# In each head, the output products of the head in front move ahead of the attend products

## Chip, cores, metric

The kernel runs on one core of one Trainium2 chip. The metric is the device time of one execution in microseconds; lower is better. The engines are named as in the profile: PE (TensorE, with PEld for its weight loads), DVE (VectorE), ACT (ScalarE), POOL (GpSimd) and SP, which here only issues transfers.

## What is computed

One transformer layer in float32: layer norm, causal attention with rotary embedding, residual; then layer norm, a mixture of experts (8 experts, the best 2 of each token) with a shared expert, residual. There are 8 sequences of 256 tokens, width 256, 16 heads of 128.

```python
x = x + attn(layernorm(x), wq, wk, wv, wo)      # x: (8, 256, 256)
x = x + moe(layernorm(x), gate_w, w1, w3, w2, sw1, sw3, sw2)

def attn(x, wq, wk, wv, wo):
    q, k, v = (einsum('bsd,dnh->bsnh', x, w) for w in (wq, wk, wv))
    q, k = rope(q) / sqrt(128), rope(k)
    logits = where(causal, einsum('bqnh,bknh->bnqk', q, k), -1e30)
    a = einsum('bnqk,bknh->bqnh', softmax(logits), v)
    return einsum('bqnh,nhd->bqd', a, wo)
```

## The kernel before

Every engine has its own stream of instructions, written out by hand, and semaphores between them; no scheduler reorders anything. An engine works through its stream in order, so what stands behind a wait waits too. To keep float32 accuracy at the speed of the fp32r format, operands are split into a high and a low part: ACT copies the rounded high part out of PSUM, DVE subtracts it to get the low part, and PE does three products (low by high, high by high, high by low; the helper `three`, L638 to L643) where one would do.

The attention stage goes through the sequences b = 0 to 7 and in each through the heads h = 0 to 15, as `sequence(b)` on each of PE, DVE, ACT and POOL. It is a software pipeline: in the turn of head h, PE does

1. `transpose_probs(h)` (L681): three transposes of the softmax rows, after `prob_done` from ACT;
2. `scores(h+2)` (L674, L641), after `qkt_lo` from POOL;
3. `project(h+4)`: q and k of that head, 12 matmuls, and half of one values unit, 3 matmuls of 512 columns; here and there a small product for the router of the sequence in front (`turn_rows` at h = 4, `gate_scores` at h = 5, `ranks` at h = 10), or the transposes of the next sequence's input (h = 11);
4. `attend(h)`: three matmuls `bank<-pt_*,v_*` (L641) and one float32 matmul of two passes, `bank<-pt_late,v_late` (L690), after `pt_lo` from DVE;
5. `output(h-1)`: six matmuls `bank<-w_*,att_*` (L641), which add the product of the head in front with `wo` to the bank of the sequence's output, after `o_lo` from DVE.

The other engines in the turn of head h, each in this order:

- ACT: `pt_late` (L1449) and `pt_hi` (L1450), the copies of the transposed probabilities; `qkt_high(h+3)` (L1425); `normalise(h+1)` (L1437, L1438), which waits for `inv_done`, DVE's reciprocal; `exps(h+2)` (L1432); a values copy in odd heads; then `att_hi` of head h (L1465), which waits for `o_ps`, the end of attend(h); then the high parts of weight pieces (`split_hi`, L1415) and the router's copies, `rows_turned` (L1494) at h = 4.
- DVE: `pt_lo` (L1038, the low part that attend(h) waits for); `rinv` (L1030); mask and maximum of head h+2 (L1026); `rope_cosines` and `rope_sines` of head h+4 (L1010, L1017); `value_lo` in every fourth head (L1035); `att_lo` of head h (L1043), which waits for `att_hi`; then the router's parts, the norms (`rows_norm`, L1142, at h = 2) and low parts of weight pieces (`split_lo`, L984, in sequence 0).
- POOL: the sum of the rope products (L472) and the low part of q and k (L1638), weight pieces, and the scatter of rows to the experts.

In heads 12 to 15 of the last sequence PE has no next sequence to project. There it takes the first products of the shared expert: `up_s(0,0)` in head 12; `up_s(0,1)` and `up_s(1,0)` in head 13; `turn_s(0)` and `up_s(1,1)` in head 14; `up_s(2,0)` and `turn_s(1)` in head 15. These stand where projections stood, ahead of `attend(h)`. ACT does the silu for them (`silu_s`, L1513) behind `att_hi`, with a load of another function table each time it changes between exp and silu. DVE does the products with the gate (`mult_s`, L1188), the low parts (L1194) and the plan of expert tiles (`plan_tiles`, L1284 to L1292) there. After head 15 follow `residual` (L1125), the last sequence's router and 39 expert tiles, then the rest of the shared expert and the sums.

Of the kernel before, what the change touches and what calls it, by code (L numbers as in the profile page):

```python
# [18 lines left out]
N, H = 16, 128  # L19
# [46 lines left out]
def build(nc, x, wq, wk, wv, wo, gate_w, w1, w3, w2, sw1, sw3, sw2, cos_t, sin_t, mask_t, ident_t,  # L66
          order_t, base_t, own_t, route_t, plan_t, zero_t, out):
    ctx = ExitStack()
    with ctx:
# [200 lines left out]
        o_lo = sem("o_lo")  # L270
# [73 lines left out]
        def wait_pieces(eng, n):  # L344

            for who in range(2):
                wait(eng, w_lo[who], lo_count(n, who))
# [116 lines left out]
        def wait(eng, s, value):  # L464

            if not isinstance(value, int) or value > 0:
                eng.wait_ge(s, value)
# [169 lines left out]
        def _(pe):  # L637
# [55 lines left out]
            def output(h):  # L693


                for t in range(ST):
                    mm = three(p_y[:, t, :], [att[h % 2][b][:, t * P:(t + 1) * P] for b in range(2)],
                               [wos(b)[:, h, :] for b in range(2)], h == 0 and t == 0,
                               h == N - 1 and t == ST - 1, more=True)
                mm.then_inc(y_ps, 1)  # L700

            def sequence(b):
                j0 = b * N
                for h in range(N):
# [47 lines left out]
                    if b is not FIRST and h in (4, 5):  # L752
                        pe.wait_ge(max_done[1], j0 + h + 3)
                        if h == 4:
                            turn_rows(b, 0)
                        if h == 5:
                            gate_scores(b, 0)
                    pe.wait_ge(pt_lo, j0 + h + 1)
                    if h % GH == 0:
                        pe.wait_ge(v_lo, b * 4 + h // GH + 1)  # L760
# [2 lines left out]
                    if b is not FIRST and h == 10:  # L763
                        pe.wait_ge(max_done[1], j0 + h + 3)
                        ranks(b, 0)
                    if h >= 1 or b is not FIRST:
                        pe.wait_ge(o_lo, j0 + h)
                        if h == 1:
                            wait(pe, resid_done, b)
                        if b is FIRST and h in (1, 5, 9, 13):  # L770
                            wait_pieces(pe, (14, 22, 30, 32)[h // 4])
                        output((h - 1) % N)
                if b is LAST:
                    pe.wait_ge(o_lo, j0 + N)
                    output(N - 1)
# [9 lines left out]
            def gate_scores(n, a):  # L785
                pe.wait_ge(xt2_cp, n)
                for t in range(ST):
                    for c in range(DC):
                        mm = pe.matmul(p_gate[a][:, t, :], xt2[:, t * DC + c, :], gate_t[:, c, :], start=c == 0,  # L789
                                       stop=c == DC - 1)  # L790
                mm.then_inc(gate_ps, 1)
# [1074 lines left out]
```

## Time and profile before

| | |
|---|---|
| median of 3 runs | 759.54 us (759.2 to 760.19) |
| the profiled execution | 760.51 us, span 758.5 us |
| busy: PE, PEld, DVE | 722.3, 683.8, 643.2 us |
| busy: ACT, POOL | 538.3, 512.7 us |
| attention stage | from about 24 us to about 614 us of the span |
| mean granted TensorE clock | 0.993 of full speed |

The page of the profile gives busy time by engine and, for each engine, how long it stood still ahead of a group of instructions and who released it. PE is above 95% busy, so the question for each wait on it is whether it stands on the path. The heads are followed in the timeline: a turn of a head is taken from the first transpose of its probabilities (`bank<-ident,work`, L681) to the next head's. A matmul's start is a good mark, its end is modelled, and matmuls overlap; 256 columns start 0.12 us apart at full clock.

### The profile page before, as it was taken

To read this page: it belongs to the slowest core of one execution; us is meant where nothing else is said; L and a number is where in the kernel's file an instruction comes from. 1 tells how busy PE (TensorE), PEld (TensorE's weight loads), DVE (VectorE), ACT (ScalarE), POOL (GpSimd) and SP (SyncE) were. 2 spreads that over 40 slices of the span, in tenths; PEclk is the share of its full clock that TensorE was granted. 3 is DMA by queue.
4 is the path that set the end of the run, shared out by engine and by line. 5 is a ranking of instruction groups with operands and counts; after the bars stand their busy time and mean duration, and the time that the engine had idled before them with its cause. 6 is when DMAs were issued, how large, how long until landed. Compare 5 with 4: busy or idle time off the path is not lost.

```text
span 758.5 us, 16245 instructions
## 1 busy us (share of the span) xinstructions
PE 722.3 (95%) x5403; PEld 683.8 (90%) x5403; DVE 643.2 (85%) x1826; ACT 538.3 (71%) x1685; POOL 512.7 (68%) x536
## 2 busy tenths in 40 slices
PE   4899999999999999999999999999999789899998
PEld 4787999999999999999999999999999678699898
DVE  6898889988998989898989988998889557588667
ACT  4788777777777777777778777777776735466574
POOL 5778567777778777877777778777766405445363
PEclk9999999999999999999999999999999999899999
DMA  6545203321332143223302321312444532344371
GB/s 204 147 157 150 96 29 112 116 103 35 122 107 93 37 137 122 72 65 131 136 27 89 126 97 35 101 47 92 175 178 161 209 104 78 112 133 134 119 277 65
DMA packets 49483, 85.91 MB, mean 113 GB/s; under 512 B 8440, under 2 KB 40152, under 8 KB 47800
## 3 DMA queue, kind: packets, MB, share of 16 engines
q1 hardware_dynamic: 45352, 73.44, 28.9%
q0 software_dynamic: 4048, 11.42, 4.2%
q8 instruction: 44, 0.72, 0.4%
q14 instruction: 39, 0.32, 0.1%
HBM read 60.12 MB, written 44.59 MB: 138 GB/s over the span
## 4 chain that ended last, share of the span: by engine, by line
PE 77%; DVE 11%; ACT 5%; POOL 3%; issue 2%; DMA 1%; SPq 0%; another core or an unknown queue 0%; POOLq 0%; DVEq 0%; ACTq 0%
PE bank L641 59%; PE bank L681 4%; PE bank L674 3%; PE bank L690 3%; DVE work L1017 3%; POOL work L472 1%; DVE work L1010 1%; PE bank L885 1%; PE bank L895 1%; PE bank L897 1%; PE bank L866 1%; ACT work L1432 1%; PE bank L789 1%; POOL qkt_lo L1638 1%; DVE work L1026 1%
## 5 line engine op out<-in xcount | busy, mean ns | idle before, releaser
L1638 POOL TENSOR_TENSOR qkt_lo<-work,qkt_hi 128x512 fp32r<-128x512 f32 x128 | 166.1, 1298 | 84.5 <-ACT qkt_hi L1425 84.5
L472 POOL TENSOR_TENSOR work<-work 128x512 f32<-128x512 f32 x127 | 165.2, 1301 | 49.1 <-DVE work L1017 46.1
L1017 DVE TENSOR_TENSOR work<-bank,sinn 64x512 f32<-64x512 f32 x256 | 176.2, 688 | 3.4
L1425 ACT CAST qkt_hi<-work 128x512 fp32r<-128x512 f32 x128 | 79.6, 622 | 97.1 <-POOL work L472 95.1
L641 PE MATMUL bank<-xnt_hi,w_lo 128*128 128x256 f32 x512 | 145.9, 285 | 2.3 <-DVE xnt_lo L1048 2.3
L641 PE MATMUL bank<-xnt_lo,w_hi 128*128 128x256 f32 x512 | 145.5, 284 | 0.0
L641 PE MATMUL bank<-xnt_hi,w_hi 128*128 128x256 f32 x512 | 145.5, 284 | 0.0
L1432 ACT ACTIVATE work<-work,bias 128x128 f32<-128x128 f32 (+1 forms) x256 | 112.7, 441 | 0.0
L1010 DVE TENSOR_TENSOR work<-bank,cosn 128x512 f32<-128x512 f32 x128 | 88.0, 688 | 18.1 <-PE bank L641 17.5
L641 PEld LDWEIGHTS bank<-xnt_hi,w_lo 128*128 128x128 f32 x512 | 98.6, 193 | 3.1 <-DVE xnt_lo L1048 3.1
L641 PEld LDWEIGHTS bank<-xnt_hi,w_hi 128*128 128x128 f32 x512 | 98.9, 193 | 0.0
L641 PEld LDWEIGHTS bank<-xnt_lo,w_hi 128*128 128x128 f32 x512 | 98.8, 193 | 0.0
L641 PE MATMUL bank<-w_hi,att_lo 128*128 128x256 f32 x256 | 83.1, 325 | 0.0
L641 PE MATMUL bank<-w_hi,xnt_hi 128*128 128x512 f32 (+1 forms) x256 | 81.5, 359 | 0.0
L1026 DVE CUSTOM_DVE_ANT_0 work<-bank,mask 128x128 f32<-128x128 f32 (+1 forms) x256 | 78.7, 345 | 1.1 <-PE bank L641 1.1
L641 PE MATMUL bank<-w_hi,xnt_lo 128*128 128x512 f32 (+1 forms) x192 | 71.9, 375 | 4.8 <-DVE xnt_lo L1182 3.5
L641 PE MATMUL bank<-w_lo,att_hi 128*128 128x256 f32 x256 | 72.5, 283 | 0.0
L641 PE MATMUL bank<-w_hi,att_hi 128*128 128x256 f32 x256 | 72.3, 282 | 0.0
L1043 DVE TENSOR_TENSOR att_lo<-bank,att_hi 128x256 fp32r<-128x256 f32 x128 | 54.1, 422 | 21.4 <-ACT att_hi L1465 18.5
L1038 DVE TENSOR_TENSOR pt_lo<-bank,pt_hi 128x256 fp32r<-128x256 f32 x128 | 53.4, 417 | 13.3 <-ACT pt_hi L1450 12.2
L681 PE MATMUL bank<-ident,work 128*128 128x128 f32 x384 | 63.1, 272 | 0.7 <-ACT work L1438 0.6
L1438 ACT ACTIVATE work<-work,rinv 128x256 f32<-128x256 f32 x128 | 63.3, 495 | 0.0
(183 smaller groups left out, 2123.8 us busy)
## 6 DMA issues: line engine op xcount, KB each, us to landing
rows_by_expert<-in_zero_t SPq DMA_DIRECT2D x17, 1028.0 KB
weights_split<-stage SPq DMA_DIRECT2D x40, 176.0 KB, 1.9
w_lo<-weights_split SPq DMA_DIRECT2D x4, 1408.0 KB
stage<-rows_by_expert SPq DMA_DIRECT2D x39, 128.5 KB
w_lo<-results_by_token SPq DMA_DIRECT2D x16, 256.0 KB, 5.5
w_hi<-weights_split SPq DMA_DIRECT2D x2, 1536.0 KB
stage<-in_L_ffn_w SPq DMA_DIRECT2D x32, 88.0 KB
weights_split<-stage SPq DMA_DIRECT2D x20, 128.0 KB, 1.9
```

What stands on the lines that cost most here:

```text
L472: eng.tensor_tensor(roped[:, a], rope_cos[:, a], rope_sin[:, a], ALU.add).then_inc(rope_add, 1)
L641: mm = pe.matmul(out, lhs[a], rhs[b], start=start and n == 0, stop=stop and n == 2, skip_group_check=more)
L681: mm = pe.transpose(p_t[:, k, :], prob[h % 2][:, k * P:(k + 1) * P], ident[:, :])
L1010: nc.vector.tensor_tensor(rope_cos[:, a], p_qk[a][:, :, :], c, ALU.mult)
L1017: op = nc.vector.tensor_tensor(rope_sin[lo:lo + 64, a], p_qk[a][hi:hi + 64, :, :], sn, ALU.mult)
L1026: nc.vector.tensor_tensor_reduce(prob[a][:, cols], p_s[a][:, t, keys], mask[:, m], -SCALE, BIG, ALU.add, ALU.min, bias[:, a, t:t + 1]).the ...
L1038: nc.vector.tensor_tensor(pts[1][:, :, :], p_t[:, 0:2, :], pts[0][:, :, :], ALU.subtract).then_inc(pt_lo, 1)
L1043: nc.vector.tensor_tensor(att[a][1][:, :], p_o[:, a, :], att[a][0][:, :], ALU.subtract).then_inc(o_lo, 1)
L1425: nc.scalar.copy(qkt[a][0][:, :, :], roped[:, a]).then_inc(qkt_hi, 1)
L1432: nc.scalar.activation(prob[a][:, c], prob[a][:, c], ACT.Exp, bias=bias[:, a, t:t + 1], scale=-1.0, accum_out=rsum[:, a, t:t + 1]).then_in ...
L1438: nc.scalar.activation(prob[a][:, P:3 * P], prob[a][:, P:3 * P], ACT.Copy, scale=rinv[:, a, 1:2]).then_inc(prob_done, 1)
L1638: nc.gpsimd.tensor_tensor(qkt[a][1][:, :, :], roped[:, a], qkt[a][0][:, :, :], ALU.subtract).then_inc(qkt_lo, 1)
```

## The change

In PE's `sequence`, the block with the wait for `o_lo` and `output(h-1)` moves from behind `attend(h)` to ahead of it and of its wait for `pt_lo`. Nothing is added or removed, and the streams of DVE, ACT, POOL and SP are the same.

```diff
@@ -755,6 +755,13 @@
                             turn_rows(b, 0)
                         if h == 5:
                             gate_scores(b, 0)
+                    if h >= 1 or b is not FIRST:
+                        pe.wait_ge(o_lo, j0 + h)
+                        if h == 1:
+                            wait(pe, resid_done, b)
+                        if b is FIRST and h in (1, 5, 9, 13):
+                            wait_pieces(pe, (14, 22, 30, 32)[h // 4])
+                        output((h - 1) % N)
                     pe.wait_ge(pt_lo, j0 + h + 1)
                     if h % GH == 0:
                         pe.wait_ge(v_lo, b * 4 + h // GH + 1)
@@ -763,13 +770,6 @@
                     if b is not FIRST and h == 10:
                         pe.wait_ge(max_done[1], j0 + h + 3)
                         ranks(b, 0)
-                    if h >= 1 or b is not FIRST:
-                        pe.wait_ge(o_lo, j0 + h)
-                        if h == 1:
-                            wait(pe, resid_done, b)
-                        if b is FIRST and h in (1, 5, 9, 13):
-                            wait_pieces(pe, (14, 22, 30, 32)[h // 4])
-                        output((h - 1) % N)
                 if b is LAST:
                     pe.wait_ge(o_lo, j0 + N)
                     output(N - 1)
```

PE, an ordinary head, from the last of its values products on. Before:

```order
L641 MATMUL bank2<-w_lo,xnt_hi 128x512
L641 MATMUL bank6<-pt_hi,v_lo0 128x256 [waits pt_lo]
L641 MATMUL bank6<-pt_hi,v_hi0 128x256
L641 MATMUL bank6<-pt_lo,v_hi0 128x256
L690 MATMUL bank6<-pt_late,v_late0 128x128
L641 MATMUL bank7<-w_hi,att_lo1 128x256 [waits o_lo]
...
L641 MATMUL bank7<-w_lo,att_hi1 128x256
L681 MATMUL bank5<-ident,work 128x128 [waits prob_done]
```

After the change:

```order
L641 MATMUL bank2<-w_lo,xnt_hi 128x512
L641 MATMUL bank7<-w_hi,att_lo1 128x256 [waits o_lo]
...
L641 MATMUL bank7<-w_lo,att_hi1 128x256
L641 MATMUL bank6<-pt_hi,v_lo0 128x256 [waits pt_lo]
L641 MATMUL bank6<-pt_hi,v_hi0 128x256
L641 MATMUL bank6<-pt_lo,v_hi0 128x256
L690 MATMUL bank6<-pt_late,v_late0 128x128
L681 MATMUL bank5<-ident,work 128x128 [waits prob_done]
```

The six products for bank 7 stood between attend and the next head's transposes; now they stand between the values product and attend, and the transposes follow attend directly.

PE, the last sequence, from the end of head 14's shared-expert product (`up_s(1,1)`, bank 1) to head 15's first transpose. Before:

```order
L641 MATMUL bank1<-w_hi,xnt_hi 128x352 x2
L641 MATMUL bank6<-pt_hi,v_lo1 128x256 [waits pt_lo]
L641 MATMUL bank6<-pt_hi,v_hi1 128x256
L641 MATMUL bank6<-pt_lo,v_hi1 128x256
L690 MATMUL bank6<-pt_late,v_late1 128x128
L641 MATMUL bank7<-w_hi,att_lo1 128x256 [waits o_lo]
...
L681 MATMUL bank5<-ident,work 128x128 [waits prob_done]
```

After the change:

```order
L641 MATMUL bank1<-w_hi,xnt_hi 128x352 x2
L641 MATMUL bank7<-w_hi,att_lo1 128x256 [waits o_lo]
...
L641 MATMUL bank6<-pt_hi,v_lo1 128x256 [waits pt_lo]
L641 MATMUL bank6<-pt_hi,v_hi1 128x256
L641 MATMUL bank6<-pt_lo,v_hi1 128x256
L690 MATMUL bank6<-pt_late,v_late1 128x128
L681 MATMUL bank5<-ident,work 128x128 [waits prob_done]
```

Here too output(13) now comes first, so attend(14) and the `o_ps` that ACT waits for stand six products later in PE's stream.

## Rows read from the trace of the kernel before

**Rows 1.** Page, part 1: busy us, share of the span, instructions.

```profile
PE 722.3 (95%) x5403; PEld 683.8 (90%) x5403; DVE 643.2 (85%) x1826; ACT 538.3 (71%) x1685; POOL 512.7 (68%) x536
```

**Rows 2.** Timeline of PE, sequence 3, head 13: start us, length, engine line operation.

```profile
305.76 0.49 PE L681 MATMUL bank<-ident,work 128*128 128x128 f32 x3
...
309.16 0.39 PE L690 MATMUL bank<-pt_late,v_late 128*128 128x128 f32 x2
...
310.09 0.39 PE L681 MATMUL bank<-ident,work 128*128 128x128 f32 x2
```

**Rows 3.** PEld's waits in 24 to 102.8, 102.8 to 579, 579 to 614: us, times, longest.

```profile
PEld bank L641 <- DVE pt_lo L1038: 7.1, 10, 1.3
...
PEld bank L641 <- DVE pt_lo L1038: 4.0, 13, 0.4
...
PEld bank L641 <- DVE pt_lo L1038: 2.6, 3, 1.3
```

**Rows 4.** Timeline of DVE, sequence 0, from head 4 to head 5.

```profile
48.39 0.41 DVE L1038 TENSOR_TENSOR pt_lo<-bank,pt_hi 128x256 fp32r<-128x256 f32 x1
...
52.45 0.91 DVE L984 TENSOR_TENSOR w_lo<-stage,w_hi 128x512 fp32r<-128x512 f32 x1
53.28 0.41 DVE L1038 TENSOR_TENSOR pt_lo<-bank,pt_hi 128x256 fp32r<-128x256 f32 x1
```

**Rows 5.** Timeline of PE and ACT in the same head; in brackets the idle time before.

```profile
48.86 0.38 PE L641 MATMUL bank<-pt_hi,v_lo 128*128 128x256 f32 x1 [0.27 <-DVE pt_lo L1038]
...
48.91 0.40 ACT L1437 ACTIVATE work<-work,rinv 128x128 f32<-128x128 f32 x1 [0.34 <-DVE rinv L1030]
...
50.75 1.23 ACT L1415 CAST w_hi<-stage 128x512 fp32r<-128x512 f32 x2
```

**Rows 6.** Timeline of DVE and PE, sequence 1, head 3.

```profile
117.10 1.47 DVE L1142 TENSOR_SCALAR xn<-resid,mv,rstd 128x256 f32<-128x256 f32 x2
118.49 0.41 DVE L1038 TENSOR_TENSOR pt_lo<-bank,pt_hi 128x256 fp32r<-128x256 f32 x1
...
118.64 0.39 PE L641 MATMUL bank<-w_lo,xnt_hi 128*128 128x512 f32 x1
...
119.18 0.28 PE L641 MATMUL bank<-pt_hi,v_hi 128*128 128x256 f32 x1
```

**Rows 7.** Timeline of PE and ACT, sequence 7, heads 5 and 6.

```profile
562.37 0.39 PE L690 MATMUL bank<-pt_late,v_late 128*128 128x128 f32 x2
...
562.79 0.37 ACT L1465 CAST att_hi<-bank 128x256 fp32r<-128x256 f32 x1 [0.78 <-PE bank L690]
...
563.83 0.27 ACT L1449 COPY pt_late<-bank 128x128 f32<-128x128 f32 x1 [0.60 <-PE bank L681]
```

**Rows 8.** Page, part 5: DVE's cosines: busy, mean ns | idle before them, releaser.

```profile
L1010 DVE TENSOR_TENSOR work<-bank,cosn 128x512 f32<-128x512 f32 x128 | 88.0, 688 | 18.1 <-PE bank L641 17.5
```

**Rows 9.** PEld's other wait in 102.8 to 579 that bears on this.

```profile
PEld bank L789 <- DVE bias L1026: 0.8, 2, 0.4
```

**Rows 10.** Timeline of PE and ACT, sequence 7, head 12.

```profile
595.02 0.39 PE L690 MATMUL bank<-pt_late,v_late 128*128 128x128 f32 x2
...
595.57 0.35 ACT L1465 CAST att_hi<-bank 128x256 fp32r<-128x256 f32 x1
```

**Rows 11.** The chain that ended last, heads 14 and 15 of sequence 7.

```profile
605.40 0.37 ACT att_hi L1465
...
609.87 0.35 DVE pt_lo L1038
...
610.25 1.01 PE bank L641 x3
...
611.69 2.16 PE bank L641 x12
```

**Rows 12.** Stretches of 2 us: busy PE, PEld, DVE, ACT, POOL, then granted PE clock.

```profile
609.00:611.00 2.00, 0.97 (x6) 0.75 (x4) 1.10 (x6) 0.00 (x0) 0.00 (x0) 0.69 0.03 8
611.00:613.00 2.00, 2.00 (x12) 2.00 (x11) 0.42 (x1) 1.16 (x4) 0.00 (x0) 0.50 0.42 129
```

## The prediction

> **What bounds the kernel now.** I read the page first: PE is busy for 722.3 of 758.5 us and DVE for 643.2 [rows 1]. A busy PE is not proof that it is the bound, so next I read the timeline of PE in an ordinary head. From head 13's first transpose to head 14's it takes 310.09 - 305.76 = 4.33 us [rows 2], and I found that value within 0.02 us in 69 of the 111 turns of sequences 1 to 7. Inside such a head the matmuls start one behind the other without a hole. Attend's float32 matmul starts at 309.16, the next transpose at 310.09, 0.93 later. Its two passes take about 0.23, so the six output products take 0.70 to 0.71, 0.118 each; attend as a whole takes 0.35 + 0.23 = 0.58. In these heads order inside PE is free of charge: the same work stands there in any order.
>
> Only a wait can be won. Then I read who waited for whom, in three stretches. PE's weight loads waited for `pt_lo` 7.1 us in 10 places while sequence 0 ran, 4.0 us in 13 places from there to head 9 of sequence 7, and 2.6 us in 3 places in the tail [rows 3]. This is the wait that the change puts 0.71 us of other work in front of, and 13.7 us is the ceiling of its gain. The reader should now ask of each whether it is PE that is late, or the others.
>
> **Sequence 0: nothing.** DVE starts `pt_lo` at 48.39 and the next at 53.28: 4.89 us, while PE's own work is 4.33. In between DVE runs almost without a hole: `pt_lo`, masks, rope, `att_lo`, the statistics of the next norm, and a weight piece of 0.91 whose high part ACT must have made before [rows 4]. ACT in turn stands on DVE's reciprocal (0.34 idle) and gets to that high part at 50.75 for 1.23 us, with no hole in between [rows 5]. So DVE and ACT go round with each other at 4.87 to 4.89 us, and no step of that round waits for PE. PE starts attend at 48.86, after 0.27 of idle weight loads [rows 5]. After the change output fills this hole, attend still starts when `pt_lo` is there, the next transposes start 0.71 us sooner, and PE waits as long again one head on. The hole moves, it does not close. What is late next is the same DVE piece. I take 0. The bounds are a gain of all 7.1 and, since 0.71 of work now goes into a hole of 4.87 - 4.33 = 0.5, a loss of 0.3, where the hole was small.
>
> **Sequences 1 to 7: 0.7 gained.** The wait comes back once in each, in head 3. DVE has two long pieces just before (the norm, 1.47 us for two, at 117.10), so `pt_lo` runs from 118.49 to 118.90; the last values product starts at 118.64 and is over at 118.88; and the second attend matmul comes at 119.18 where 118.64 + 0.24 + 0.12 = 119.00 would do [rows 6]. That is 0.2 us of PE time, seven times, 1.4 us; all are of the same size. Output's 0.71 covers it each time, if nothing else gets late.
>
> What does get late is `att_hi`. It starts 0.42 behind the float32 matmul (562.37 to 562.79), which was 0.52 ahead of the next transposes; ACT then idled 0.60 and took `pt_late` at 563.83, 0.53 behind the transposes [rows 7]. After the change, with output no longer in between, `att_hi` comes 0.42 - 0.23 = 0.19 behind the transposes, ends at 0.56, and `pt_late` at 0.53 is late by nothing to speak of. So in a plain head ACT has just the room. Where ACT was already later than that (up to 0.7 behind the transposes, as it is after a values copy) nothing changes. Where a router copy or a weight piece stands between `att_hi` and `pt_late`, these push `pt_late`, `pt_hi` and `pt_lo` up to 0.3 later. `pt_lo` can afford it: attend is now needed 0.71 later. DVE's idle before its cosines, where it waits for PE's projections, swallows much of the rest: 17.5 us over the 128 heads [rows 8]. The one place that has no such cover is head 5: `gate_scores` stands ahead of output and waits for DVE's maximum, 0.8 us in two places already [rows 9]. With PE 0.2 sooner and DVE 0.1 later I expect that wait in three of the sequences, so about half of the 1.4 is given back. I take a gain of 0.7. Bounds: a gain of all 4.0; or a loss of 2, if ACT's delay reaches PE by 0.3 in each sequence.
>
> **The tail: 0.9 lost.** The three `pt_lo` waits here [rows 3] are in heads 10, 11 and 15, where DVE's plan of tiles makes it late; it does not wait for PE, so filling them wins nothing by itself. In heads 12 to 15 of the last sequence PE is often idle and latency decides. The chain that ended last runs through ACT's `att_hi` of head 14 at 605.40, a function table, the silu, DVE's products and its plan, `pt_lo` of head 15 at 609.87, attend at 610.25, twelve output products from 611.69 to 613.85 [rows 11]. Output(13) used to run behind attend(14), in the shadow of ACT; now it stands ahead of it and behind `up_s(1,1)`, so `att_hi(14)` and all that follows come 0.71 later. The same happens in head 12: the float32 matmul was at 595.02, `att_hi` could have started at 595.44 and did at 595.57 [rows 10]. Now it starts at 595.02 + 0.71 + 0.42 = 596.15, 0.58 later, with silu and table load behind it. In head 13 the delay of attend is hidden, since ACT has a table load and exponentials to do before it comes to `att_hi`. So attend(15) starts at 610.25 + 0.58 + 0.71 = 611.54.
>
> Something comes back at the end. Output(14) now lies in the wait ahead of attend(15). Behind attend(15) only output(15) is left, but now it must wait for `att_hi` and `att_lo` openly. PE's clock stood at 0.69 of full in 609 to 611, when PE was busy for 0.97 us only, and at 0.50, 1.2 GHz, in 611 to 613 [rows 12]. At that clock attend's three matmuls took 1.01 [rows 11]. With another 0.5 to `att_hi`, 0.37 for it, 0.42 for `att_lo` (as long as `pt_lo`, of the same shape) and half of 2.16 for six products I get 3.4 from attend(15) to the end of output(15). At full clock it is 0.36 to the float32 matmul, 0.42 to `att_hi` [rows 7], 0.83 for the two copies and 0.87 for six products with the end of the last one: 2.5. Before, attend and twelve products took 613.85 - 610.25 = 3.60 [rows 11]. So the tail loses 1.29 - 0.2 = 1.1 or 1.29 - 1.1 = 0.2. I take 0.9, near the half clock, because PE's pause between the transposes of head 15 and `up_s(2,0)`, which waits for ACT's silu, grows by the 0.71 that output(14) no longer fills. The range is 0.2 to 1.5.
>
> The Trainium skill ("TensorE: Matmul & The Clock Gate", "Why this matters for your kernels") tells one to avoid idle gaps between bursts of matmuls, since the clock falls behind them. This trace agrees: 0.50 behind the pauses. By that rule a filled wait ahead of attend(15) might keep the clock up, and the tail would lose 0.2; the sum would end 0.7 us lower.
>
> What comes after the attention stage (residual, router of the last sequence, 39 tiles) hangs on output(15), so a shift there is passed on as it is.
>
> **The sum.** -0.7 + 0 + 0.9 = +0.2 us on the profiled execution's 760.51. That one is 1.0 above the median of 759.54; I put the same shift on the median: 759.7, rounded with the open end of the tail to 759.8.
>
> **Rivals.** (1) *The waits are real.* If DVE and ACT are held back by PE after all, so that a head of sequence 0 gets shorter when PE is sooner, 0.5 us of PE time in each of nine heads is won, 4.5, and 1.4 in the rest: 759.54 - 5.9 + 0.9 gives 754.5; half of the gain, 757.5. For it: all the waits have one releaser. Against: DVE's round of 4.89 has hardly a hole [rows 4]. Chance 0.17 for a gain that can be measured. (2) *The delay of `att_hi` gets through* in the steady part: ACT's order puts the next head's `pt_late` and `pt_hi` behind it, DVE's `att_lo` is followed by `pt_lo`. It decides from the point where ACT is more than about 0.3 us late at the transposes, since it then has no idle 0.60 [rows 7] left; it is so in heads with a copy behind `att_hi`. At one such head per sequence with 0.6 us passed on, seven give 4.2, and with the tail's 0.9 and no gain in head 3 that is 764.6; with half of it 762.5. Chance 0.22. (3) *The clock stays up* in the tail: 759.0, inside "no change". (4) That the change doesn't do what it says is excluded; the streams are written by hand and their order shows the move.
>
> **Chances.** A measurement of this kernel can tell about 0.2%, 1.5 us, from no change. Forecast and rival (3): 0.60. Faster by more: 0.18. Slower by more: 0.22. For eight in ten the range reaches halfway into rivals (1) and (2): 757.4 to 762.8.
>
> **What the profile would show.** Right: transposes directly behind the float32 matmul; head 3 of sequences 1 to 7 at 4.33 instead of 4.53; heads 2 to 6 of sequence 0 still at about 4.87, their wait now split between `prob_done` and `pt_lo`; `att_hi` never less than 0.19 behind the next transposes; `pt_lo` of head 15 some 1.3 us later relative to head 11. Wrong: shorter heads in sequence 0 (rival 1); any steady head above 4.33 that was not so before (rival 2); or a tail in which attend(14) is not 0.7 later, because ACT was late for another reason.

## The result, and the profile after

| | before | with the change |
|---|---|---|
| median of 20 runs each, on one chip | 760.32 us (758.06 to 763.2) | 761.82 us (760.13 to 763.88) |
| ratio, 95% interval | | 1.0021 [1.0012, 1.003] |
| profiled execution: time, span | 760.51, 758.5 | 760.13, 758.1 |
| mean granted clock of the profiled execution | 0.993 | 0.993 |

The change costs 1.5 us. The interval of the ratio leaves 1 out, but it has the 0.2% in it that the prediction took for the edge of what can be told from no change. The profiled pair says something else: there the changed kernel is 0.4 us faster. Its profiled execution is the fastest of the 20, and both statements are right. How, is the main lesson of this case.

First the page of the changed kernel (as in [rows 1] and [rows 8]: busy us, share, instructions; then busy and mean ns | idle before, releaser):

```profile
PE 722.8 (95%) x5403; PEld 686.6 (91%) x5403; DVE 639.0 (84%) x1826; ACT 541.0 (71%) x1685; POOL 512.7 (68%) x536
...
L1043 DVE TENSOR_TENSOR att_lo<-bank,att_hi 128x256 fp32r<-128x256 f32 x128 | 54.1, 423 | 35.0 <-ACT att_hi L1465 32.3
```

The work is the same. DVE's `att_lo` now waits longer for `att_hi` (32.3 us in all, where the page of before has 18.5), because attend, whose result `att_hi` is copied from, now stands last in each head.

PE in the plain head, sequence 3, head 13 (timeline; [rows 2] before):

```profile
305.44 0.49 PE L681 MATMUL bank<-ident,work 128*128 128x128 f32 x3
...
309.54 0.39 PE L690 MATMUL bank<-pt_late,v_late 128*128 128x128 f32 x2
309.76 0.49 PE L681 MATMUL bank<-ident,work 128*128 128x128 f32 x3
```

The next transposes stand directly behind the float32 matmul, 0.22 later, and the head still takes 309.76 - 305.44 = 4.32.

PEld's waits in sequence 0, then from there to 579, then in the tail to 614 (us, times, longest; [rows 3] and [rows 9] before):

```profile
PEld bank L681 <- ACT work L1438: 3.5, 10, 1.3
PEld bank L641 <- DVE pt_lo L1038: 1.4, 4, 0.8
...
PEld bank L789 <- DVE bias L1026: 2.0, 6, 0.5
...
PEld bank L641 <- DVE att_lo L1043: 1.1, 1, 1.1
...
PEld bank L641 <- DVE pt_lo L1038: 0.2, 1, 0.2
```

The wait for `pt_lo` fell from 7.1 to 1.4 in sequence 0, from 4.0 to nothing that the list shows in the middle, and from 2.6 to 0.2 in the tail: 13.7 us of wait became 1.6. Hardly any of it became time. In sequence 0 2.4 us of the wait turned up at the next head's transposes (1.1 before, 3.5 now), and where the rest went the list does not show; in the middle 1.2 us of new wait stand at `gate_scores` (six places, before two). In the tail there is a new wait for `att_lo`, and the waits ahead of the shared expert's products grew: that for `xnt_lo` (L1182) from 2.8 to 3.8, and PE's pause ahead of `up_s(2,0)` from 1.29 to 2.00.

Sequence 0, DVE's `pt_lo` of two heads in a row, as in [rows 4]:

```profile
48.72 0.41 DVE L1038 TENSOR_TENSOR pt_lo<-bank,pt_hi 128x256 fp32r<-128x256 f32 x1
...
53.61 0.41 DVE L1038 TENSOR_TENSOR pt_lo<-bank,pt_hi 128x256 fp32r<-128x256 f32 x1
```

4.89 apart, exactly as before. The sum of its 16 heads is 78.50 us (before 78.56). Single heads did move: heads 1, 2 and 8 got shorter by 0.31, 0.17 and 0.51, heads 7 and 12 longer by 0.48 and 0.42, and it cancels out.

Heads of sequences 1 to 7, from transposes to transposes, after minus before: head 3 -0.20 to -0.22, seven times; head 10 -0.17 to -0.26, and -0.50 in the last sequence; given back in head 5 (+0.05 to +0.19, in six sequences), head 1 (+0.04 to +0.07 in three), head 11 (+0.05) and head 12 (+0.07 to +0.19, in front of the last sequence). Head 3 is [rows 6] without its hole. Head 10 nobody had foretold: PE in sequence 1, before,

```profile
151.65 0.25 PE L801 MATMUL bank<-member,order 128*128 128x8 f32 x1
151.76 0.36 PE L641 MATMUL bank<-w_hi,att_lo 128*128 128x256 f32 x1
151.97 0.28 PE L641 MATMUL bank<-w_hi,att_hi 128*128 128x256 f32 x1
```

and with the change

```profile
150.82 0.28 PE L641 MATMUL bank<-w_hi,att_lo 128*128 128x256 f32 x1
150.93 0.28 PE L641 MATMUL bank<-w_hi,att_hi 128*128 128x256 f32 x1
...
152.36 0.25 PE L801 MATMUL bank<-member,order 128*128 128x8 f32 x1
152.47 0.55 PE L681 MATMUL bank<-ident,work 128*128 128x128 f32 x3
```

The first output product held PE for 0.21 when it followed `ranks`, and holds it for 0.11 behind a values product.

From the first transposes to `pt_lo` of head 11 of sequence 7 it is 563.21 us, before 564.61: **1.4 us gained**. This is one pair of executions. Over the profiles of the experiments below (light_output left out, whose clock fell in this stretch) the same stretch takes 564.61 to 566.11 us in the six with the old order in sequences 1 to 7, mean 565.4, and 563.21 to 564.61 in the five with the new one, mean 564.0. The gain is of that size, but two executions of one order can differ by as much.

The tail, PE, ACT and DVE of the changed kernel ([rows 10] and [rows 11] before):

```profile
594.66 0.39 PE L690 MATMUL bank<-pt_late,v_late 128*128 128x128 f32 x2
...
605.66 0.37 ACT L1465 CAST att_hi<-bank 128x256 fp32r<-128x256 f32 x1 [1.65 <-PE bank L690]
...
607.95 0.40 PE L641 MATMUL bank<-w_hi,xnt_lo 128*128 128x352 f32 x1 [2.00 <-ACT work L1513]
...
610.04 0.42 DVE L1038 TENSOR_TENSOR pt_lo<-bank,pt_hi 128x256 fp32r<-128x256 f32 x1
...
611.85 0.48 PE L690 MATMUL bank<-pt_late,v_late 128*128 128x128 f32 x2
...
613.25 0.39 PE L641 MATMUL bank<-w_hi,att_lo 128*128 128x256 f32 x1 [0.92 <-DVE att_lo L1043]
...
614.26 0.69 DVE L1125 TENSOR_TENSOR resid<-resid,bank 128x512 f32<-128x512 f32 x1 [1.07 <-PE bank L641]
```

From `pt_lo` of head 11 (587.80) to the residual it is 26.46 us, before 25.00 (588.87 to 613.87): **1.46 lost**. Stretches of 2 us of the same place ([rows 12] before):

```profile
608.00:610.00 2.00, 2.00 (x10) 1.92 (x11) 1.90 (x9) 0.67 (x4) 0.00 (x0) 0.66 0.03 8
610.00:612.00 2.00, 2.00 (x11) 2.00 (x11) 0.46 (x2) 0.00 (x0) 0.00 (x0) 0.50 0.03 5
612.00:614.00 2.00, 1.08 (x9) 0.89 (x8) 0.42 (x1) 1.16 (x4) 0.00 (x0) 0.99 0.54 160
```

The clock fell to 1.2 GHz behind the pause of 2.0 us that PE makes ahead of `up_s(2,0)` (1.29 before). Counted from `pt_lo` of head 11 it fell where it did before, 20.8 us behind (20.9 before), but the work is 1.3 us later there. So output(14) ran at half clock and pushed attend(15) past the `pt_lo` that was there at 610.46: attend(15) starts at 611.21, 23.41 behind `pt_lo` of head 11, where before it was 610.25 - 588.87 = 21.38. That is 2.03 later. From attend(15) to the residual it is then 3.05 us, before 3.62, since output(15) runs at full clock again; 2.03 - 0.57 = 1.46.

The start of the first head (+0.33), -1.40, +1.46 and what stands behind the residual (143.9 us to the end of the span, before 144.6) make up the 0.4 of the two profiles. It leaves the 1.5 us of the medians open. A hint is in the list of runs, which has a mean granted clock for each of the changed kernel's: of its 20 runs eight are at 0.993 (median 760.6), six at 0.991 (761.8), five at 0.989 (763.4), one at 0.988. The profiled one is of the first kind. The first kind is close to the median before; for the 20 runs before no clocks are listed.

### The profile page after: what moved, and what is told of

The parts are those of the page before. It is cut to its first block, busy times and chain, and to the rows that moved or that the text cites. A ratio compares the mean times of both kernels' runs of the same rounds, so it can differ in the third digit from the quotient of the medians.

```text
span 758.1 us, 16245 instructions
## 1 busy us (share of the span) xinstructions
PE 722.8 (95%) x5403; PEld 686.6 (91%) x5403; DVE 639.0 (84%) x1826; ACT 541.0 (71%) x1685; POOL 512.7 (68%) x536
## 4 chain that ended last, share of the span: by engine, by line
PE 80%; DVE 9%; ACT 5%; issue 2%; POOL 2%; DMA 1%; SPq 1%; DVEq 0%; POOLq 0%; ACTq 0%
PE bank L641 61%; PE bank L681 5%; PE bank L690 3%; PE bank L674 3%; DVE work L1017 2%; PE bank L895 1%; PE bank L897 1%; PE bank L866 1%; PE bank L885 1%; DVE work L1010 1%; PE bank L789 1%; POOL work L472 1%; DVE w_lo L984 1%; ACT work L1432 1%; PE bank L834 1%
## 5 line engine op out<-in xcount | busy, mean ns | idle before, releaser
L1010 DVE TENSOR_TENSOR work<-bank,cosn 128x512 f32<-128x512 f32 x128 | 87.8, 686 | 15.9 <-PE bank L641 15.5
L1043 DVE TENSOR_TENSOR att_lo<-bank,att_hi 128x256 fp32r<-128x256 f32 x128 | 54.1, 423 | 35.0 <-ACT att_hi L1465 32.3
L641 PE MATMUL bank<-w_hi,att_lo 128*128 128x256 f32 x256 | 74.1, 289 | 0.9 <-DVE att_lo L1043 0.9
L1465 ACT CAST att_hi<-bank 128x256 fp32r<-128x256 f32 x128 | 47.0, 367 | 32.3 <-PE bank L690 27.9
```

The source lines that it names most:

```text
L641: mm = pe.matmul(out, lhs[a], rhs[b], start=start and n == 0, stop=stop and n == 2, skip_group_check=more)
L1010: nc.vector.tensor_tensor(rope_cos[:, a], p_qk[a][:, :, :], c, ALU.mult)
L1043: nc.vector.tensor_tensor(att[a][1][:, :], p_o[:, a, :], att[a][0][:, :], ALU.subtract).then_inc(o_lo, 1)
L1465: nc.scalar.copy(att[h % 2][0][:, :], p_o[:, h % 2, :]).then_inc(o_hi, 1)
```

## The experiments

The theories: **theory 1**, that of the prediction: nothing to gain in sequence 0, little in head 3, and a tail whose price is ACT's late `att_hi` of heads 12 and 14. Its **rival 1**: the waits are real and shorter heads give the gain. After the first eight runs came **theory 2**: the tail's price is that lateness and, beside it, a granted clock that falls in more places per execution. (In the expectations of the first four runs "theory 2" still stands for another one, the prediction's rival 2: ACT's later `att_hi` gets through in ordinary heads.) All twelve were timed against the kernel before, which ran beside them. Their edits are one function and a condition; the changed kernel is the condition "always".

```
+            def add_output_of_last(b, h):
+                if h >= 1 or b is not FIRST:
+                    pe.wait_ge(o_lo, b * N + h)
...
+                    output((h - 1) % N)
...
+                    if early(b, h):
+                        add_output_of_last(b, h)
                     pe.wait_ge(pt_lo, j0 + h + 1)
...
+                    if not early(b, h):
+                        add_output_of_last(b, h)
```

| kernel | new order in | median, us | before beside it | ratio, 95% |
|---|---|---|---|---|
| all_but_tail | all but heads 12 to 15 of the last sequence | 757.02 | 757.67 | 0.9994 [0.9981, 1.0007] |
| tail_only | heads 12 to 15 of the last sequence | 761.68 | 757.67 | 1.0066 [1.0046, 1.0086] |
| seq0_only | sequence 0 | 757.87 | 757.67 | 1.0002 [0.999, 1.0014] |
| steady_only | sequences 1 to 7 without that tail | 756.43 | 757.67 | 0.9989 [0.9977, 1.0001] |
| whole_change | everywhere | 760.64 | 758.23 | 1.0034 [1.0021, 1.0047] |
| heads_12_14 | heads 12 and 14 of the last sequence | 761.31 | 758.23 | 1.0045 [1.0029, 1.0061] |
| head_15 | head 15 of the last sequence | 758.55 | 758.23 | 1.0002 [0.9988, 1.0015] |
| heads_3_10 | heads 3 and 10 of sequences 1 to 7 | 757.06 | 758.23 | 0.998 [0.9966, 0.9993] |
| whole_filled | everywhere, idle PE filled in the tail | 759.93 | 760.51 | 0.9992 [0.9981, 1.0002] |
| heads_3_10_filled | heads 3 and 10, idle PE filled in the tail | 759.45 | 760.51 | 0.9979 [0.9968, 0.9989] |
| head_14 | head 14 of the last sequence | 761.17 | 760.51 | 1.0005 [0.9993, 1.0017] |
| light_output | nowhere; lighter output in sequence 0 | 761.09 | 760.51 | 1.0003 [0.9989, 1.0017] |

The first four, the next four and the last four ran on a chip each. The times of the kernel before differ between these chips by up to 2.8 us, so a kernel is to be held against the one before beside it. Microseconds below that are said to be "by the ratio" are the ratio times that median.

### The change in parts

`early` is `not (b is LAST and h >= 12)`.

> The new order everywhere but in heads 12 to 15 of the last sequence, which keep the old one. Theory 1 (the tail pays, the rest gains): the profiled pair showed about 1.4 us gained by the start of the tail and about 1.4 lost in it, so this kernel is 1.0 to 1.5 us faster than before, ratio near 0.998, and its tail from DVE's pt_lo of head 11 to the end of output(15) takes about 25.0 us as before. Theory 2 (the later att_hi gets through in the ordinary heads in many executions): at least 1 us slower than before, ratio 1.001 or more, and the tail alone changes nothing.

0.6 us less, interval -1.4 to +0.5. Theory 1 had 1.0 to 1.5 less; the side fits, but no change at all is not excluded. The rival's loss of 1 us or more is excluded. Its profile has 24.34 from `pt_lo` of head 11 to the residual, where before has 25.00 with 0.8 of half clock at its end.

`early` is `b is LAST and h >= 12`.

> The new order only in heads 12 to 15 of the last sequence. Theory 1: slower than before by 1.4 to 3 us, ratio 1.002 to 1.004, with attend(14) 0.7 later and output(14) at half clock ahead of attend(15). Theory 2: within 0.5 us of before.

4.0 us more by the medians, 5.0 by the ratio, interval 3.5 to 6.5 (six runs only). Theory 1 had the side and the place right and the size wrong. Its profile has 26.46 from `pt_lo` of head 11 to the residual, 1.46 more than before, just as the changed kernel; the rest must lie outside that stretch, or in executions that are not like the profiled one. Part of it lies behind the residual, as the table in the section on the clock shows.

`early` is `b is FIRST`.

> The new order only in sequence 0. Theory 1: DVE and ACT set the pace there, so the first transposes of sequence 1 come within 0.3 us of before and the time is the same within 0.3 us. Rival (the waits for pt_lo are real): 2 us or more faster.

0.2 us more, interval -0.8 to +1.1: nothing. In its profile sequence 0 takes 78.56 us, as before. This speaks against rival 1.

`early` is `b is not FIRST and not (b is LAST and h >= 12)`.

> The new order in sequences 1 to 7 without the tail. Theory 1: 1.0 to 1.5 us faster than before (head 3 from 4.53 to 4.33, head 10 from 4.87 to 4.69, 0.1 given back in heads 5 and 12). Theory 2: slower than before by 1 us or more.

0.8 us less by the ratio, interval -1.7 to +0.1. Theory 1 had 1.0 to 1.5 less. Heads 3 and 10 are shorter by 0.2 each as in the changed kernel, heads 5 and 12 longer.

### Is the wait of sequence 0 real?

Here five of the six output products are left out in heads 2 to 9 of sequence 0, the order is the old one:

```
-            def output(h):
+            def output(h, light=False):
+                if light:
+                    pe.matmul(p_y[:, 0, :], att[h % 2][0][:, 0:P], wos(0)[:, h, :], start=False, stop=False,
+                              skip_group_check=True).then_inc(y_ps, 1)
+                    return
...
-                        output((h - 1) % N)
+                        output((h - 1) % N, light=b is FIRST and 2 <= h <= 9)
```

> The old order, with five of the six output products left out in heads 2 to 9 of sequence 0, so that heads 1 to 8 of that sequence are missing from the product with wo, except for one matmul each. This takes 0.59 us of PE's work out of each of eight heads. Theory 1 (DVE and ACT go round at 4.87 to 4.89 and no step of that round waits for PE): heads 4 to 6 of sequence 0 stay at 4.87 to 4.89, the sequence is shorter by less than 0.5 us. Rival 1 (the waits are real, PE holds the round back): those heads fall to 4.4 or so, 3 to 4 us less in the sequence and in the kernel.

PEld's wait for `pt_lo` in sequence 0 grew from 7.1 to 9.9 us, and DVE's `pt_lo` of two heads in a row stand as far apart as ever (53.43 - 48.55 = 4.88):

```profile
PEld bank L641 <- DVE pt_lo L1040: 9.9, 10, 1.8
```

```profile
48.55 0.41 DVE L1040 TENSOR_TENSOR pt_lo<-bank,pt_hi 128x256 fp32r<-128x256 f32 x1
53.43 0.41 DVE L1040 TENSOR_TENSOR pt_lo<-bank,pt_hi 128x256 fp32r<-128x256 f32 x1
```

The sequence takes 78.57 us, before 78.56, with 8 x 0.59 = 4.7 us less work on PE. Heads 2 and 8 got 0.5 shorter, heads 7 and 10 0.5 longer again; heads 4 to 6 did not move. The whole kernel took 0.2 us more, interval -0.8 to +1.3. Rival 1 is refuted: PE was spared 4.7 us in the stretch that holds 7.1 us of waits, and none of it became time.

### Where the tail's price sits

The whole change once more, on the chip of the next three:

> The whole change once more, beside its parts on one chip. Its parts gave, each alone: heads 12 to 15 of the last sequence 4.0 us more than before, sequences 1 to 7 without that tail 1.2 less, sequence 0 nothing (0.2 more). Theory 1 (costs of parts add up, what moves is order alone): 2 to 3 us above before, and above heads_12_14 and head_15 in its share. Rival (the tail's price depends on when the tail falls, so it is lower in the whole change than alone): within 1 us of before.

2.6 us more by the ratio, interval 1.6 to 3.6. That is a little above the result's 1.5. Costs of parts do not add up: the three parts timed on the first chip make 5.0 + 0.2 - 0.8 = 4.4.

`early` is `b is LAST and h in (12, 14)`.

> The new order only in heads 12 and 14 of the last sequence. Output(11) and output(13) now stand ahead of attend(12) and attend(14), and nothing stands open behind attend(15) that did not before. Theory 1: att_hi of head 12 0.58 later, that of head 14 0.71 more, attend(15) 1.3 us later, and from pt_lo(7,15) to the residual nothing changes (3.25 at full clock, 4.09 at half): 1.3 us more than before, 1 to 2 with the clock. Rival (the price of the tail is the open wait behind attend(15) and not ACT's late att_hi): nothing, within 0.4 of before.

3.4 us more by the ratio, interval 2.2 to 4.6 (eight runs): all of the price and more. The rival, a price in the open wait at the end, falls. Theory 1 had 1.3, 1 to 2 with the clock, and that is too small as well.

`early` is `b is LAST and h == 15`.

> The new order only in head 15 of the last sequence: output(14) fills the wait ahead of attend(15), and output(15) has to wait for att_hi and att_lo in the open. Theory 1: attend(15) starts when it did, from pt_lo(7,15) to the residual 0.9 to 1.0 longer at the same clock (4.22 against 3.25), so 0.2 to 1.0 us more than before. Rival (the price of the tail is att_hi of heads 12 and 14 alone, and the filled wait keeps the clock up): 0 to 0.5 less than before.

0.2 us more, interval -0.9 to +1.1. Theory 1's 0.9 to 1.0 for the open wait was wrong. Its DVE rows, `pt_lo`, `att_lo` and residual:

```profile
612.39 0.42 DVE L1047 TENSOR_TENSOR pt_lo<-bank,pt_hi 128x256 fp32r<-128x256 f32 x1
614.14 0.42 DVE L1052 TENSOR_TENSOR att_lo<-bank,att_hi 128x256 fp32r<-128x256 f32 x1 [1.34 <-ACT att_hi L1474]
615.64 0.69 DVE L1134 TENSOR_TENSOR resid<-resid,bank 128x512 f32<-128x512 f32 x1 [1.07 <-PE bank L641]
```

3.25 us with the new order, and seq0_only, steady_only and heads_3_10 have 3.25 with the old one. The 4.22 that I had put down to the open wait was the half clock: the old order has 4.09 at half clock too (before, 609.78 to 613.87).

`early` is `b is LAST and h == 14`.

> The new order only in head 14 of the last sequence. Theory 1: att_hi of head 14, and with it silu, plan and attend(15), 0.71 later, so 0.7 us more than before by lateness. Theory 2: PE's pause ahead of up_s(2,0) grows by that 0.7 too (1.3 to 2.0), so the clock falls once more and falls in the tiles too: 2 to 3 us more, nearly all of heads_12_14's 3.1, with a mean clock of 0.993 to 0.996 in the runs. If the price sits in head 12: within 0.5 of before.

0.4 us more, interval -0.5 to +1.3; so lateness alone (0.7) fits and theory 2's 2 to 3 are excluded. `pt_lo` of head 15 comes 21.63 behind that of head 11, 0.67 more than the 20.96 of the undisturbed old order (heads_3_10_filled, below): the 0.71 of the prediction. PE's pause ahead of `up_s(2,0)` is 2.00 long, and in the profile the clock stands at half for 6.8 us behind it, twice as long as elsewhere; the runs' mean clock is 0.9918, before 0.9931. The big price does not come from head 14 alone, at least on this chip.

### The clock

Theory 2 rests on a reading across all profiles. In each of those without fillers there are one to three spells at 1.2 GHz between the start-up and the last tiles: one in the tail (between 593 and 618), often one in the tiles (around 655), in heads_12_14 two in the tail, in light_output one at 276. Read from the granted clock each lasts 3.4 us or 6.8. One of 3.4 us at half clock takes 1.7 of 758 us from the mean clock, 0.0023: about the step between 0.993, 0.991 and 0.989 in the list of runs above. To test it, PE gets matmuls to do in its pauses, with results that nobody reads:

```
+            def fill(out, count):
+                for n in range(count):
+                    pe.matmul(out, wos(0)[:, N - 1, 0:P], wos(0)[:, N - 1, :], start=True, stop=True)
...
                         if h == 12:
+                            pe.wait_ge(v_lo, B * 4)
+                            pe.wait_ge(v_hi, B * 8)
+                            fill(p_v[:, 0:D], 12)
                             up_s(0, 0)
...
                         if h == 14:
+                            fill(p_s[0][:, 0, :], 12)
                             turn_s(0)
...
                         if h == 15:
+                            fill(p_s[0][:, 0, :], 8)
                             up_s(2, 0)
```

> The whole change, and in its tail idle PE gets something to do: 12 matmuls of output's shape ahead of up_s(0,0) in head 12, 12 ahead of turn_s(0) in head 14, 8 ahead of up_s(2,0) in head 15, into PSUM that nobody reads then (their results are thrown away). At 0.118 each they fill 1.4, 1.4 and 0.9 of pauses of 1.8, 2.0 and 1.3 to 2.1. Theory 2 (the tail's price is 1.3 of lateness, and the rest is a granted clock that falls once more per execution): the clock stays at 1.0 from 590 to 620, the mean clock of the runs goes from 0.995 to 0.998 or above, and the kernel takes 0 to 1 us more than before in place of 2.4. Rival (the clock is no cause, lateness of DVE and ACT is all): 2.4 us more than before, as without the fillers, or more.

0.6 us less than before by the ratio, interval -1.4 to +0.2, where the whole change without the fillers took 2.6 more on another chip (whole_change) and 1.5 more in the result. By these differences 32 useless matmuls save 2 to 3 us. Their stretches, to be held against those of the changed kernel above:

```profile
608.00:610.00 2.00, 1.58 (x11) 1.59 (x12) 1.65 (x6) 1.14 (x5) 0.00 (x0) 1.00 0.00 0
610.00:612.00 2.00, 1.50 (x11) 1.10 (x9) 0.87 (x5) 0.13 (x1) 0.00 (x0) 1.00 0.00 0
612.00:614.00 2.00, 1.24 (x9) 1.25 (x10) 0.65 (x2) 1.03 (x4) 0.00 (x0) 1.00 0.52 132
```

The granted clock stays at 1.00, 2.4 GHz, through the tail; in the tiles it still stands at half for 6.8 us, as in all four kernels of this chip. Over its 12 runs the mean clock is 0.9959 and that of the kernel before on the same chip 0.9931 (theory 2 had 0.998 or above); without fillers the change had gone the other way, 0.9950 against 0.9973 (one run of before, at 0.946, left out). The Trainium skill ("TensorE: Matmul & The Clock Gate", "Why this matters for your kernels") tells one to avoid idle gaps between bursts of matmuls; the traces of the change and of whole_filled agree, with a granted clock of 0.50 behind the pause of 2.00 us ahead of `up_s(2,0)` and of 1.00 where 8 matmuls stand in it. The whole change without fillers did not run on this chip, and as shown below its price may differ by chip, so the 2 to 3 us are not shown. What is measured on one chip: the filled whole change is not slower than before beyond 0.2 us, and its median of 759.93 is below the 761.17 of head_14, which has only a part of the change and no fillers.

> The new order in heads 3 and 10 of sequences 1 to 7 alone, which took 1.2 us less than before, with the same 32 filling matmuls in heads 12, 14 and 15 of the last sequence. Theory 2: the one fall of the clock in that tail goes too, worth up to 1.7 us of PE time of which about half is on the path: 2 us less than before, mean clock 0.998 to 1.0. Rival (the fall costs nothing where latency decides, and fillers delay what stands behind them): 1.2 less or nothing.

1.6 us less, interval 0.8 to 2.4. Theory 2 had 2. Heads_3_10 without fillers, on another chip, has 1.5 less, interval 0.5 to 2.6. So for the old order the ratios show no share of the fillers, though in the profiles the stretch from `pt_lo` of head 11 to the residual is 24.22 us with them and 25.62 without.

The same kernel without fillers; `early` is `b is not FIRST and h in (3, 10)`.

> The new order only in heads 3 and 10 of sequences 1 to 7, the two that got shorter in the changed kernel (4.53 to 4.33, and 4.87 to 4.69), and the old order in heads 1, 5, 11 and 12, which got longer by 0.04 to 0.1 each. Theory 1 (the gain is made in those two heads, and what is given back is made where the new order delays ACT's att_hi behind the transposes): 7 x (0.20 + 0.18) = 2.7 us less than before, heads 1, 5, 11 and 12 as before. Rival (what heads 3 and 10 win is given back in the next wait, whatever the order there): 1.2 us less or nothing, with heads 5 and 11 longer as in the changed kernel.

1.5 us less, where theory 1 had 2.7 and its rival 1.2 or nothing. Held against head_15, the same chip's old order, the gain is in those two heads: head 3 is shorter by about 0.20 seven times, head 10 by 0.15 to 0.25 and by 0.48 in the last sequence. Head 1 stays as before, but head 11 (+0.05 or more) and head 12 (+0.06 to +0.10 in five sequences) give back although their order is the old one, and head 5 does so in three sequences. So part of what is given back does not come from the new order of the head itself: the next wait takes it.

The tail and what stands behind it, from the profiled executions, us. The last column says how far behind `pt_lo` of head 11 the clock fell; each fall lasts 3.4 us but for head_14's.

| kernel | chip | order in heads 12 to 15 | `pt_lo`(11) to `pt_lo`(15) | to the residual | residual to the end | clock falls at |
|---|---|---|---|---|---|---|
| heads_3_10_filled | 3rd | old | 20.96 | 3.26 | 144.3 | never |
| before | result's | old | 20.91 | 4.09 | 144.6 | 20.9 |
| all_but_tail | 1st | old | 21.09 | 3.25 | 141.2 | 6.1 |
| light_output | 3rd | old | 21.46 | 3.26 | 144.0 | 5.6 |
| steady_only | 1st | old | 22.20 | 3.26 | 141.2 | 4.6 |
| seq0_only | 1st | old | 22.24 | 3.25 | 141.2 | 14.8 |
| heads_3_10 | 2nd | old | 22.37 | 3.25 | 140.4 | 14.7 |
| head_15 | 2nd | new in 15 | 21.99 | 3.25 | 140.4 | 5.0 |
| head_14 | 3rd | new in 14 | 21.63 | 4.52 | 144.2 | 21.0, for 6.8 |
| whole_filled | 3rd | new | 22.30 | 3.25 | 144.1 | never |
| the change | result's | new | 22.24 | 4.22 | 143.9 | 20.8 |
| whole_change | 2nd | new | 22.26 | 4.21 | 142.9 | 20.4 |
| tail_only | 1st | new | 22.24 | 4.22 | 143.0 | 20.8 |
| heads_12_14 | 2nd | new in 12 and 14 | 23.79 | 3.82 | 142.6 | 5.0 and 22.1 |

Two lines have no fall in the tail: 22.30 - 20.96 = **1.34 us** is what the order alone costs there. The others show what a fall costs, by where it lies: 1.3 to 1.4 in head 14 (14.7 and 14.8), 0.8 to 1.0 at attend and output of head 15 (20.4 to 20.9). In head 12 it cost 0.1 at 6.1, 0.5 at 5.6, 1.0 at 5.0 and 1.2 at 4.6: a shift by 1.5 us moves the price by 1.1.

The column behind the residual shows a second price. On the first and second chip the three kernels with the new order in heads 12 and 14 take 142.6 to 143.0 us there, the five others 140.4 to 141.2. The difference arises in one place, about 38 us behind the residual, where PE waits for the rows of an expert tile. whole_change, then heads_3_10 on the same chip:

```profile
653.23 0.69 PE L866 MATMUL bank<-ident,stage 128*128 128x128 f32 x2 [2.64 <-DMA stage<-rows_by_expert]
...
654.00:656.00 2.00, 2.00 (x9) 1.93 (x9) 0.42 (x1) 0.61 (x2) 0.00 (x0) 0.50 0.57 131
```

```profile
652.15 0.44 PE L875 MATMUL bank<-ident,stage 128*128 128x128 f32 x2 [1.28 <-DMA stage<-rows_by_expert]
...
654.00:656.00 2.00, 2.00 (x14) 1.84 (x13) 1.60 (x5) 1.26 (x6) 0.28 (x1) 1.00 0.41 110
```

In all three the clock falls behind this wait (2.56, 2.64 and 2.30 us), in the five others, whose waits here are 1.2 to 2.3, it does not. On the third chip and in the result's pair the clock falls in the tiles whatever the order, and no kernel stands out (143.9 to 144.6). That would explain why tail_only and heads_12_14 cost so much on their chips while head_14 on the third costs 0.4. It is one profile of each kernel, and why the wait for the rows is longer there is not shown.

## Why the prediction was right, and where it was not

The forecast was 759.8 us on the median of 759.54, 0.2 more, inside "no change"; the result is 1.5 more on 760.32, with an interval of 0.9 to 2.3 more that leaves the forecast's 0.2 out. The time of 761.82 lies inside the range of 757.4 to 762.8.

- **Sequence 0: 0.** Right, and for the reason given. The waits are split as the prediction said, heads 4 to 6 stay at 4.87 to 4.89, and with 4.7 us of PE's work removed the sequence does not move. Heads 2 and 3 were not at 4.87, as the prediction has it: head 3 has 5.48 in both kernels, head 2 went from 4.87 to 4.70.
- **Head 3, 1.4 us gained.** Right: 4.53 to 4.33, seven times.
- **Half of it given back at head 5.** The place was right, `gate_scores` waits 2.0 us in six places where it waited 0.8 in two. But two pieces were missing from the sum. Head 10 wins another 0.17 or more each time: 0.10 of it is the first output product's, 0.04 the wait for `pt_lo`, the rest lies in `ranks`. And head 12 gives back 0.07 to 0.19, which the prediction did not name: the first product with the next sequence's `xnt` there holds PE longer (0.20 in place of 0.12 in sequence 1). Sequences 1 to 7 gain 1.4 us in the trace instead of 0.7; timed alone, 0.8 [-0.1 to 1.7].
- **`att_hi` 0.19 behind the transposes, and no measurable loss from it in steady heads (against rival 2).** The first half is right: in the last sequence the head is at 4.33 and `att_hi` 0.20 behind the transposes (PE and ACT, against [rows 7]):

```profile
562.05 0.39 PE L690 MATMUL bank<-pt_late,v_late 128*128 128x128 f32 x2
562.27 0.49 PE L681 MATMUL bank<-ident,work 128*128 128x128 f32 x3
...
562.47 0.37 ACT L1465 CAST att_hi<-bank 128x256 fp32r<-128x256 f32 x1 [1.21 <-PE bank L690]
```

But the prediction's own sign of being wrong, a steady head above 4.33 that was not so before, did appear in small, above all in head 12, which went from 4.33 to between 4.40 and 4.53 in five sequences. It is not rival 2: with the old order in that head (heads_3_10) it still grows by 0.06 to 0.10, and steady_only as a whole was not slower but 0.8 us faster [-0.1 to 1.7].

- **Attend(15) 1.29 later (0.58 and 0.71).** Right for `pt_lo` of head 15, which attend(15) waits for, and for attend(15) itself as long as the clock stays up: 1.34 by the two filled kernels, 0.67 for head 14 alone. In the profiled pair attend(15) is 2.03 later, because output(14), which the prediction put into the wait, ran at half clock and did not fit.
- **"Something comes back at the end", 0.2 or 1.1.** This step failed. At one clock nothing comes back between `pt_lo` of head 15 and the residual: 3.25 with the new and 3.26 with the old order at full clock, 4.22 and 4.09 with a fall there. The 1.1 came from holding six products at full clock against twelve at half. With that the tail is 1.3 to 1.5 in place of 0.9.
- **The clock.** It was priced for one place, as a choice between two values at the end. That it can fall in more places with the change had no term. Where whole_change and before ran on one chip, the mean clock of the runs is 0.002 lower with the change (0.9950, 0.9973), and the changed kernel's own runs show what that goes with: 760.6 us at 0.993, 761.8 at 0.991. That is the likely term that turns -1.4 and +1.4 into 1.5 us more. It is an accounting from medians and not shown by a run; what is shown is that filling PE's pauses removes the fall in the tail from the trace, and that the filled change is not slower than before beyond 0.2 us.
- That the sum came out inside the range is in part luck: a gain too small by 0.7 and a tail too small by 0.5 lie against each other, and a clock term of about 1 to 1.5 that it lacked was small enough.

Open stays what the parts cost in all executions: heads 12 and 14 alone (3.4) more than the whole change (2.6), the whole tail alone the most (5.0, six runs), head 14 alone 0.4. Their mean clocks rank alike where they share a chip (0.9920 for heads_12_14, 0.9950 for whole_change). The table above names two places where profiles differ, the fall in head 12 and the wait for rows in the tiles. What sets the moment of a fall no run tests.

## What to carry to other kernels

A wait that a profile lists is worth what the releaser could do sooner, not what it lasts: of 13.7 us of wait in the places that this order filled, 1.4 became time in the trace. Moving work ahead of a wait moves it behind nothing, so look for who reads the result that is now later; here it was ACT, twice, in the one stretch where latency decides. And where the question is 0.2%, compare distributions and mean clocks, not two profiles: the profiled pair had the sign wrong. Of the kernels run here the best against its own before is the new order in heads 3 and 10 alone, 0.2% with or without the fillers.

## What the runs showed of the chip

A pause of PE between bursts can cost twice: once itself, and once by the half clock behind it, whose price hangs on where it lies (0.1 to 1.4 us for 3.4 us at half clock in this tail). All twelve profiles without fillers have a spell at 1.2 GHz in the tail, where PE's longer pauses are 1.0 to 2.2 us, and neither of the two with them has. Work whose results are thrown away can keep the clock up there; that it pays for itself in the median is not shown.

The tiles have a disturbance that goes with the chip and not with the change. In before and the change, and in all four of the third chip, PE's transposes of the 14th tile's rows come 18.5 to 18.6 us behind DVE's last write of `base`, in the others 15.9 to 17.1. In the kernel before ACT stands still there for 1.68 us with no releaser, and then for 2.55 us, the last 0.7 of them behind the end of PE's product for it; the clock falls meanwhile, at 650.7:

```profile
648.26 0.37 ACT L1525 CAST qkt_hi<-bank 128x256 fp32r<-128x256 f32 x1 [1.68 <-issue]
651.18 0.32 ACT L1529 ACTIVATE work<-bank 128x176 f32<-128x176 f32 x1 [2.55 <-PE bank L641]
```

```profile
650.00:652.00 2.00, 0.52 (x4) 0.24 (x4) 0.47 (x2) 0.82 (x4) 0.00 (x0) 0.68 0.55 188
652.00:654.00 2.00, 2.00 (x7) 1.40 (x8) 1.85 (x7) 0.91 (x4) 0.89 (x1) 0.50 0.29 70
```

What holds ACT there was not tested. It is one more reason to set a kernel only against a kernel before that ran beside it.
